# Edge scores of a graph attention layer: one-hots in 2 bytes, node scores as three 2-byte pieces

## The reference, cut

```python
def gat_conv(x, src, dst, edge_attr, W, att_src, att_dst, W_e, att_e, bias, n_nodes):
    xp = (x @ W).reshape(-1, Hh, C)
    a_src = jnp.einsum('nhc,hc->nh', xp, att_src)
    a_dst = jnp.einsum('nhc,hc->nh', xp, att_dst)
    a_edge = edge_attr @ w_e
    alpha = jax.nn.leaky_relu(a_src[src] + a_dst[dst] + a_edge, 0.2)
    m = jax.ops.segment_max(alpha, dst, num_segments=n_nodes)
    ex = jnp.exp(alpha - m[dst])
    denom = jax.ops.segment_sum(ex, dst, num_segments=n_nodes)
    msg = xp[src] * (ex / (denom[dst] + 1e-16))[:, :, None]
    return jax.ops.segment_sum(msg, dst, num_segments=n_nodes).reshape(n_nodes, Hh * C) + bias
```

## Time and profile before

| | |
|---|---|
| time, median of 3 runs | 3224.36 us (3220.84 to 3227.27) |
| the profiled execution: time, span | 3225.35 us, 3223.5 us |
| TensorE matmul / weight load busy | 2658.5 us (82%) / 2315.1 us (72%) |
| VectorE busy | 2145.0 us (67%) |
| ScalarE busy | 1174.6 us (36%) |
| GpSimd busy | 1899.9 us (59%) |
| mean granted TensorE clock | 0.827 of full |
| DMA, all queues | 489.16 MB, 152 GB/s |

### The profile page before, as it was taken

The page is one execution under the profiler, slowest core; times in us unless marked ns, Lnnn a source line. Parts: engine busy times, 40 slices in busy tenths (PEclk is TensorE's granted clock), DMA queues, the critical chain, the costliest instruction groups (busy, mean ns, idle before and its releaser), DMA issues. The chain is left out here.

```text
span 3223.5 us, 76668 instructions
## 1 busy us (share of the span) xinstructions
PE 2658.5 (82%) x15653; PEld 2315.1 (72%) x15654; DVE 2145.0 (67%) x5435; ACT 1174.6 (36%) x4700; POOL 1899.9 (59%) x1991
## 2 busy tenths in 40 slices
PE   6689999899999999996888878888877756688897
PEld 4578788787787877865777777777777635677786
DVE  6476676666666666664777777777777655555565
ACT  3243443444344334452333333333333542222222
POOL 2466666666666666416777777777777224055564
PEclk9777777777777777797999989999998858599999
DMA  8655555555555555325666666666666247344433
GB/s 263 186 151 142 138 153 136 140 153 134 143 148 138 146 144 139 98 80 152 176 172 175 175 174 176 174 176 174 173 175 175 66 145 256 96 141 150 130 116 92
DMA packets 521893, 489.16 MB, mean 152 GB/s; under 512 B 295959, under 2 KB 431277, under 8 KB 521828
## 3 DMA queue, kind: packets, MB, share of 16 engines
q0 software_dynamic: 96384, 285.57, 31.9%
q1 hardware_dynamic: 354324, 149.37, 18.1%
q10 hardware_dynamic: 71120, 53.52, 5.3%
HBM read 406.96 MB, written 81.21 MB: 151 GB/s over the span
## 5 line engine op out<-in xcount | busy, mean ns | idle before, releaser
L666 POOL DMA_INDIRECT e_rows<-table,e_idx x1664 | 1576.3, 947 | 728.5 <-issue 405.5
L1029 PE MATMUL e_ps_sum<-e_hot,e_msg 128*128 128x129 f32 x6656 | 1190.0, 321 | 233.2 <-DVE e_msg L705 162.3
L1029 PEld LDWEIGHTS e_ps_sum<-e_hot,e_msg 128*128 128x128 f32 x6656 | 994.5, 220 | 374.2 <-ACT parts L902 224.0
L901 ACT ACTIVATE acc<-e_ps_sum 128x256 f32 x1664 | 639.2, 384 | 1384.2 <-PE e_ps_sum L1029 1191.2
L705 DVE TENSOR_TENSOR e_msg<-e_rows,e_ps_pr 128x256 f32<-128x256 f32 x1664 | 660.2, 416 | 111.0 <-PE e_ps_pr L1022 46.0
L1012 PEld LDWEIGHTS e_ps_al<-e_win,e_hotT 128*128 128x128 f32 x3328 | 481.3, 223 | 7.5 <-DVE e_hotT L696 7.5
L1012 PE MATMUL e_ps_al<-e_win,e_hotT 128*128 128x8 f32 x3328 | 473.8, 270 | 6.8 <-DVE e_hotT L696 6.8
L686 DVE TENSOR_TENSOR e_hot<-e_ps_pr,rel 128x512 f32<-128x512 f32 x416 | 286.5, 689 | 225.9 <-PE e_ps_sum L1029 192.2
L696 DVE TENSOR_TENSOR e_hotT<-e_relb,e_ps_pr 128x512 f32<-128x512 bf16 x416 | 281.8, 677 | 1.4 <-PE e_ps_al L1012 1.0
L902 ACT ACTIVATE parts<-e_ps_sum 128x4 f32 (+1 forms) x1664 | 279.6, 168 | 0.0
L1918 ACT ACTIVATE x_h<-x,eb 128x128 f32<-128x128 f32 x216 | 67.4, 363 | 274.8 <-PE x L1987 274.8
(11 more groups left out here) (294 smaller groups left out, 3221.0 us busy)
## 6 DMA issues: line engine op xcount, KB each, us to landing
e_relb<-rel_rows SPq DMA_DIRECT2D x104, 512.0 KB, 5.1
e_win<-table SPq DMA_DIRECT2D x1664, 4.0 KB
e_rows<-table,e_idx POOLq DMA_INDIRECT x1664
e_eattr<-in_edge_b SPq DMA_DIRECT2D x104, 128.0 KB
e_xT<-turned_x ACTq DMA_DIRECT2D x100, 128.0 KB
e_xr<-in_x ACTq DMA_DIRECT2D x100, 128.0 KB
node<-acc SPq DMA_DIRECT2D x25, 512.0 KB, 3.8
table<-t_row ACTq DMA_DIRECT2D x25, 272.0 KB, 4.2
```

The costliest lines, as they stand in the source:

```text
L666: nc.gpsimd.indirect_dma_start(out=rows[q][:, k, :], out_offset=None, in_=table, in_offset=bass.IndirectOffsetOnAxis(ap=idx[:, q, k:k + 1] ...
L901: nc.scalar.activation(acc[:, :, bass.ds(at[k], P)], ps_sum[(k + q) % 3][:, :, 0:P], ACT.Copy).then_inc(s["window"], 1)
L1029: op = nc.tensor.matmul(ps_sum[(k + q) % 3][:, a, 0:WIN], msg[:, k % RM, a * P:a * P + P], hot[:, q, k, :], start=(a == 0), stop=True, ski ...
```

## The change

A table row becomes TW = 276 floats: columns 264 to 275 hold, in place of the 8 destination scores, three 2-byte pieces of each (24 values): the score rounded to bf16, what that leaves rounded to bf16, and what is left then. `pieces_of` makes them with five elementwise instructions of 8 columns a row: on GpSimd behind each block's copy in `first` and in layer 0's `join`, and on VectorE for the 832 joined rows. The table's store moves from ScalarE's queue to SP's in `first`, and in both stages it waits for the split. In `edges`, `hotT` is bf16, `win` holds the 24 pieces, and the product of a tile is one of 2-byte operands with 24 columns. `leaky` reads the three pieces from PSUM with three additions in place of one.

```diff
 ROW = F + 2 * H
+NPC = 3 * H
+TW = F + H + NPC // 2
...
-        table = [nc.dram_tensor(f"table{l}", (NP, ROW), F32).ap() for l in range(2)]
+        table = [nc.dram_tensor(f"table{l}", (NP, TW), F32).ap() for l in range(2)]
...
+def pieces_of(eng, row, high, rest):
+
+    exact, parts = row[..., F + H:ROW], row[..., F + H:TW].bitcast(BF16)
+    eng.tensor_copy(high, exact)
+    eng.drain()
+    eng.tensor_tensor(rest, exact, high, ALU.subtract)
+    eng.drain()
+    eng.tensor_copy(parts[..., H:2 * H], rest)
+    eng.tensor_copy(parts[..., 0:H], high)
+    eng.drain()
+    return eng.tensor_tensor(parts[..., 2 * H:NPC], rest, parts[..., H:2 * H], ALU.subtract)
...
-        row = tmp("row", [P, 2, 2, ROW])
+        row = tmp("row", [P, 2, 2, TW])
...
+                if n >= 2:
+                    store(n - 2)
...
+            store(NCH - 2)
+            store(NCH - 1)
...
+            def split(n):
+                pool.wait_ge(s["rowc"], n + 1)
+                pieces_of(nc.gpsimd, row[:, n % 2], high[:], rest[:]).then_inc(s["split"], 1)
...
             for n in range(NCH):
-
+                if n >= 3:
+                    split(n - 3)
                 pool.wait_ge(s["mv"], n + 1)
                 nc.gpsimd.tensor_tensor(rstd[:, 2 * n:2 * n + 2], epsb[:, 2 * n:2 * n + 2], cst[:, 0:1].broadcast_to((P, 2)),
...
+            for n in range(NCH - 3, NCH):
+                split(n)
...
-                    op = nc.scalar.activation(row[:, n % 2, b, :], ps_row[n % 2][b][:, 0:ROW], ACT.Copy)
+                    op = nc.scalar.activation(row[:, n % 2, b, 0:ROW], ps_row[n % 2][b][:, 0:ROW], ACT.Copy)
                 op.then_inc(s["rowc"], 1)
-                act.wait_ge(s["rowc"], n + 1)
-                act.dma_start(table[n * CH:n * CH + CH, :].rearrange("(b p) f -> p b f", p=P), row[:, n % 2]
-                              ).then_inc(s[f"out{n % 2}"], 16)
...
-        rows = [tmp(f"rows{q}", [P, GT, ROW]) for q in range(2)]
-        win = tmp("win", [P, 2, GT, H])
+        rows = [tmp(f"rows{q}", [P, GT, TW]) for q in range(2)]
+        win = tmp("win", [P, 2, GT, NPC // 2])
...
-        hotT = tmp("hotT", [P, 2, 4, P])
+        hotT = tmp("hotT", [P, 2, 4, P], BF16)
...
+        parts_al = ps_al[:, 0:NPC * GT].rearrange("p (k x) -> p k x", k=GT)
+        turned_al = ps_al[:, NPC * GT:NPC * GT + P]
...
-                    sp.dma_start(win[:, q, k, :], table[bass.ds(at, P), F + H:ROW]).then_inc(s[f"win{q}"], 16)
+                    sp.dma_start(win[:, q, k, :], table[bass.ds(at, P), F + H:TW]).then_inc(s[f"win{q}"], 16)
...
-                nc.vector.tensor_tensor(al[:].rearrange("p (k h) -> p k h", h=H),
-                                        ps_al[:, 0:P].rearrange("p (k h) -> p k h", h=H), rows[q][:, :, F:F + H], ALU.add)
-                vec.drain()
+                by_tile = al[:].rearrange("p (k h) -> p k h", h=H)
+                nc.vector.tensor_tensor(by_tile, parts_al[:, :, 0:H], rows[q][:, :, F:F + H], ALU.add)
+                vec.drain()
+                for j in range(1, 3):
+                    nc.vector.tensor_tensor(by_tile, parts_al[:, :, j * H:j * H + H], by_tile, ALU.add)
+                    vec.drain()
                 nc.vector.scalar_tensor_tensor(lr[:], al[:], 0.2, al[:], ALU.mult, ALU.max).then_inc(s["leaky"], 1)
...
-                nc.vector.tensor_tensor_scan(peak[:], mark[:, q, 0, 0:P], ps_al[:, P:2 * P], -BIG, ALU.add, ALU.max)
...
                     for a in range(2):
-                        nc.tensor.matmul(ps_al[:, 64 * a:64 * a + 64], eattr[:, q, a, :],
-                                         wedge[:, layer].rearrange("p b h -> p (b h)"), start=(a == 0), stop=False,
+                        nc.tensor.matmul(parts_al[:, H * a:H * a + H, 0:H], eattr[:, q, a, :],
+                                         wedge[:, layer], start=(a == 0), stop=False,
                                          skip_group_check=True)
...
-                    m = H * (4 * r + k)
-                    op = nc.tensor.matmul(ps_al[:, m:m + H], hotT[:, r % 2, k, :], win[:, q, 4 * r + k, :], start=False,
+                    m = 4 * r + k
+                    op = nc.tensor.matmul(parts_al[:, m, :], hotT[:, r % 2, k, :], win[:, q, m, :].bitcast(BF16), start=False,
                                           stop=(r == 3 and k == 3), skip_group_check=True)
...
-                nc.tensor.transpose(ps_al[:, P:2 * P], lr[:], ident[:]).then_inc(s["turned"], 1)
+                nc.tensor.transpose(turned_al, lr[:], ident[:]).then_inc(s["turned"], 1)
...
-    WIDTH = ROW if layer == 0 else F
+    WIDTH = TW if layer == 0 else F
+    MADE = ROW if layer == 0 else F
...
-                sp.wait_ge(s["rowc"], n + 3)
+                sp.wait_ge(s["split" if layer == 0 else "rowc"], n + (1 if layer == 0 else 3))
...
+                def split(n, q):
+                    pool.wait_ge(s["rowc"], n + 3)
+                    pool.nop(nofuse=True)
+                    pieces_of(nc.gpsimd, row[:, q], high[:], rest[:]).then_inc(s["split"], 1)
+
+                with pool.Fori(0, HALF) as i:
+                    split(2 * i, 0)
+                    split(2 * i + 1, 1)
+                split(NCH - 1, 0)
...
-                pool.wait_ge(s["fixc"], f + 1)
+                if layer == 0:
+                    pool.wait_ge(s["fixs"], 1 + (f == NFIX - 1))
+                else:
+                    pool.wait_ge(s["fixc"], f + 1)
...
+            if layer == 0:
+                f, n = NFIX - 1, T - (NFIX - 1) * P
+                vec.wait_ge(s["fixc"], f)
+                pieces_of(nc.vector, fix[:, 0:f], fix_high[:, 0:f], fix_rest[:, 0:f]).then_inc(s["fixs"], 1)
+                vec.wait_ge(s["fixc"], NFIX)
+                pieces_of(nc.vector, fix[0:n, f], fix_high[0:n, f], fix_rest[0:n, f]).then_inc(s["fixs"], 1)
```

More of the change, by code:

```diff
@@ L163, in first @@
         hT = tmp("hT", [P, 2, 2, CH])
-        row = tmp("row", [P, 2, 2, ROW])
+        row = tmp("row", [P, 2, 2, TW])
+        high = tmp("high", [P, 2, H], BF16)
+        rest = tmp("rest", [P, 2, H])
         att1 = tmp("att1", [P, 2, F])
@@ L195, in first @@
         names = ("w", "x0", "x1", "x2", "x3", "iota", "mv", "rstd", "xn", "turned", "copied", "rectified", "row", "rowc",
-                 "xo0", "xo1", "out0", "out1", "edge_in", "dst_in", "marks_in", "att_in", "cols_in", "kq_in", "v_in", "src_in",
+                 "split", "xo0", "xo1", "out0", "out1", "edge_in", "dst_in", "marks_in", "att_in", "cols_in", "kq_in", "v_in", "src_in",
                  "rel", "rel_t", "rel_c", "marks", "bvb", "wv_t", "wv_c", "product", "stored")
@@ L222, in fetch, with store @@
                              ).then_inc(s[f"x{n % 4}"], 16)
+            def store(n):
+                sp.wait_ge(s["split"], n + 1)
+                sp.dma_start(table[n * CH:n * CH + CH, :].rearrange("(b p) f -> p b f", p=P), row[:, n % 2]
+                             ).then_inc(s[f"out{n % 2}"], 16)
             for n in range(4):
@@ L243, in _ @@
                                      mk[:].rearrange("p r m e -> p r (m e)")).then_inc(s["stored"], 16)
+            store(NCH - 2)
+            store(NCH - 1)
+            for q in range(2):
+                sp.wait_ge(s[f"out{q}"], 16 * (NCH // 2 + (q == 0)))
             sp.wait_ge(s["stored"], 16 * 10)
@@ L466, in _ @@
             rows(NCH - 1)
-            for q in range(2):
-                act.wait_ge(s[f"out{q}"], 16 * (NCH // 2 + (q == 0)))
         @block.tensor
@@ L731, in highest @@
                 vec.wait_ge(s["turned"], g + 1)
-                nc.vector.tensor_tensor_scan(peak[:], mark[:, q, 0, 0:P], ps_al[:, P:2 * P], -BIG, ALU.add, ALU.max)
+                nc.vector.tensor_tensor_scan(peak[:], mark[:, q, 0, 0:P], turned_al, -BIG, ALU.add, ALU.max)
                 vec.drain()
@@ L738, in less_highest @@
                 vec.drain()
-                nc.vector.tensor_tensor(less[:], ps_al[:, P:2 * P], seg[:], ALU.subtract).then_inc(s["less"], 1)
+                nc.vector.tensor_tensor(less[:], turned_al, seg[:], ALU.subtract).then_inc(s["less"], 1)
                 nc.vector.tensor_copy(ends[:, bass.ds(g, 1), :, 0:1].rearrange("p a b c -> p (a b c)"), seg[:, 0:P:P - 1])
@@ L1171, in join @@
         fix = tmp("fix", [P, NFIX, WIDTH])
+        high = tmp("high", [P, 2, H], BF16)
+        rest = tmp("rest", [P, 2, H])
+        fix_high = tmp("fix_high", [P, NFIX, H], BF16)
+        fix_rest = tmp("fix_rest", [P, NFIX, H])
         ps = [pb(f"j{layer}_{q}", [P, 512], ctx) for q in range(4)]
@@ L1174, in join @@
         names = ("pick", "picked", "less", "ex", "weight", "inv", "spread", "taken", "total", "hT", "row", "rowc",
-                 "out0", "out1", "fixT", "fix", "fixc", "put", "on")
+                 "out0", "out1", "fixT", "fix", "fixc", "fixs", "split", "put", "on")
         s = {n: sem(f"j{layer}_{n}", ctx) for n in names}
@@ L1312, in rows @@
                 for k in range(2):
```

(4 more changed lines are left out.)

## The result

The changed kernel takes 3170.55 us (median of 4 runs, 3169.48 to 3175.33) where the kernel before took 3225.82 beside it (4 runs, 3220.84 to 3227.41): a ratio of 0.9837, 95% interval 0.9821 to 0.9854. It is 55 us faster. The forecast was 3089, 136 us faster.

The account below looks back on a forecast made before the run. GpSimd's 1.25 us gathers were taken to bound layer 1, TensorE at half clock to hold layer 0. Terms -153 - 2 + 0 + 9 + 4 + 6 = -136 on 3225.35, less 1.0 for the median, gave 3089 us, range 3050 to 3120.

Parts of the forecast that it names:

- The reading: Edge stages: layer 0 is 172 us slower than layer 1 though ScalarE and GpSimd have less load per us there.
- The bound: Edge layers: gathers 1.25 us apart make a floor of 1038.8 us; layer 0 lay 187.8 above it, layer 1 16.7.
- TensorE's work: Edge groups: 16 lighter score records save 2.3 us a group at full clock (1.6 to 3.2), 4.5 at half.
- The step that failed: Layer 0: with 12.1 us of TensorE work at full clock, a 20.0 us group needs a granted clock of 0.60.
- the 35 us left above the floor: Layer 0's gathers: 35 us expected above the 1038.8 us floor after the change, between 0 and 187.8.
- -153: Layer 0's gathers: change of -153 us, with bounds of -188 and, at 21.5 us a group, -110.
- VectorE becomes the pace: Rival, layer 0: VectorE sets 21.5 us a group, waiting for `keys`; kernel at 3132 us; chance 0.13.
- The clock's rival: Layer 0: TensorE pauses more and gets half clock throughout; kernel slower, 3249 to 3301 us; chance 0.06.
- Layer 1: Layer 1's gathers stay at their floor: 0 us, bounds -17 and +16.
- +9 forecast: Stage `first`: table stores wait for the splits, +9 us, bounds 0 and +45.
- +4 forecast: Layer 0's join, row loop: 4.1 us a pair of blocks against 3.75, +4 us over 12 pairs, bounds 0 and +47.
- a rival, priced at 20 to 40 us: Join: splits cost several times 1.2 us beside VectorE's scans, 20 to 40 us by the shared-port rule; chance 0.13.

Follow-up runs that it names:

- x_fill: Changed kernel with twelve unread fp32 products a group put into TensorE's pauses in layer 0: 3102.36 us.
- b_fill_4: Kernel before the change, whole, with twelve unread products a group in layer 0: 3058.18 us, ratio 0.9475 to the kernel before.
- x_one_add: Changed kernel without the two additions over the second and third pieces in `leaky`, both layers: 3135.5 us, ratio 0.9724 to the kernel before.
- x_ring: Changed kernel with GpSimd's power ahead of the split in `first` and five row buffers in layer 0's join in place of two: 3146.96 us.

## Why the prediction was wrong

**The reading.** One sentence of it is wrong: ScalarE has more load per us in layer 0 than in layer 1, not less (501.67 of 1257.1 us against 392.40 of 1085.1); GpSimd and VectorE have less. Nothing was worked out from it.

**The bound.** Right: 1.25 us a gather is the floor, and layer 0's distance to it is TensorE's clock. `x_fill` and `b_fill_4` reach it, with 16.3 and 23.0 us above.

**TensorE's work.** Right in size. The new records take 0.11 us for four tiles (807.34 to 807.45) where the old took 0.81, so 2.8 us a group at full clock; I had 2.3, between 1.6 and 3.2, and 0.05 to 0.06 us a record where it is 0.028.

**The step that failed** is "20.0 us need only 3.8 us of full clock, a clock of 0.60", and with it the 35 us left above the floor, where 90.8 are left. The clock is 0.76, well above it, and a group takes 21.7 us. A mean says nothing here. The lighter work turned into pauses (TensorE's waits for messages went from 55.4 to 121.7 us), and the half clock lies on the two steps that VectorE waits for, in 40 of 48 groups where it was 23; full clock during a stretch in which TensorE waits for messages gives nothing back. So -153 became -97. The bound that I had written beside it, -110 at 21.5 us a group, was short by 13. With the half clock filled away (`x_fill`) the same work is done in 16.3 us above the floor.

**VectorE.** The rival "VectorE becomes the pace" was nearest for layer 0: 21.5 us a group forecast, 21.7 found. But it named `keys` as the place (now 10.3 us), and it is the key sums and the turned probabilities; and it isn't VectorE's work alone, as `x_fill` shows: the same work of VectorE fits into 20.3 us a group. Both hold at once: with these waits in the way each us of VectorE's work costs about a us (`x_one_add`); with the waits gone `b_fill_4`, which lacks the two additions, is no faster in layer 0 than `x_fill`.

**The clock's rival** had the mechanism (less work, more pauses, half clock) and the wrong size: it needed a clock below 0.57 to make the kernel slower. I gave it 0.06 and added nothing for it to the likeliest case. The Trainium skill (TensorE: Matmul & The Clock Gate, The HAM clock gate) lets activity release the clock; `x_fill` agrees: more activity, 0.92 in place of 0.77. I had called that rule borne out only in part, because layer 1 has more pauses and the higher clock. After the change layer 1, lighter too, went from 0.90 to 0.85.

**Layer 1.** Right: 0 forecast, +2.2 measured.

**`first`.** +9 forecast, +13.4 measured, by another way. I worked out the store's delay; the order on GpSimd (split ahead of the power) was in the diff, and I didn't name who waits behind it. That costs 8.9 of the 13.4 (`x_ring`), so that +9 came near is luck.

**The join.** +4 forecast for the row loop, +25.6 measured. Two terms were too small. A pair of undisturbed blocks was to take 4.1 us and takes 4.76 to 4.87, where it was 3.75: about 12 us over 12 pairs in place of 4, with a split of 1.38 us in place of 1.2 and a store that lands after 2.5 in place of 2.2. And the scans were left to a rival, priced at 20 to 40 us; by this rest and the estimate above they are 12 to 15. Behind the loop +6 forecast, +8.3 measured; ahead of it -2 and -6.6.

In all, layer 0 is 56 us short, the join's row loop 22 and `first` 4; the other terms cancel to within 1 us. These are the 81.5 us between 3089 and 3170.55.

## What to carry to other kernels

Before an engine with a granted clock is given less to do, look at where it pauses and what it does right behind the pause: if that is what others wait for, lighter work can be given back there, and cheap unread products in the pauses may be worth more than the change itself (172 us against 55 here, but nothing on three other chips, where other waits held the kernel). A mean clock or a mean load doesn't show this; the clock by stretches within one group does. And where small GpSimd instructions read SBUF in a stage in which VectorE has long instructions with two SBUF inputs, price them at VectorE's length, or give their buffers enough depth. Where a kernel's times differ from run to run, look first which of them the trace shows: here the fastest of four made two additions look worth 50.5 us, and the median 41.

## What was not expected of the hardware

2-byte products of 128x24 come 0.028 us apart, four in 0.11 us, and of 128x8 0.025 apart (12 in 0.30): the number of columns hardly counts at this size. More work made TensorE faster: with 24 more records a group the same sums were done at a clock of 0.92 in place of 0.77, and with them in the heavier kernel of before at 0.97 in place of 0.75. Less work made the half clock come more often: at the turn of the probabilities in 40 of 48 groups in place of 23, though each time for less long.
